# The fourth attention's result norms taken in three groups inside its steps, and a tile of the last layer cleared later

## What is computed

```
x = x + tanh(g_xattn[3]) * _L3_xattn_ref(_layernorm(x), ctx, ctx, mask, gamma, beta)
x = x + tanh(g_ffn[3])   * _L3_ffn_ref(_layernorm(x), Wg, bg, Wi, Wo, A, B)

def _L3_xattn_ref(q, k, v, mask, gamma, beta):
    logits = where(mask == 0, -9e15, q @ k.T / sqrt(d_k))
    x = softmax(logits) @ v
    mu, var = mean(x), mean((x - mu)**2)          # per token, over the 256 features
    return (x - mu) * rsqrt(var + 1e-5) * gamma + beta

def _L3_ffn_ref(x, ...):
    # softmax over 4 experts, the two best; one shared base x @ Wi and a rank-4 term per expert,
    # relu, @ Wo, weighted by the two scores
```

## Time and profile before

| | |
|---|---|
| median of 3 runs | 1665.69 us (1663.48 to 1671.44) |
| the profiled execution | 1655.67 us, of it 1653.8 us from the first to the last instruction |
| TensorE, busy share | 84% (weight loads 71%) |
| VectorE, ScalarE, GpSimd, busy share | 69%, 57%, 46% |
| instructions | 31758 |
| mean granted TensorE clock | 0.923 of full |

### The profile page before, as it was taken

How to read it: one execution, slowest core, us unless ns; L and a number is a source line. 1 busy time by engine, 2 the same in 40 slices (tenths; PEclk the granted TensorE clock), 3 DMA queues, 4 the chain that set the end, 5 groups by cost and what they waited for, 6 DMA issues and landing times. The chain is left out here.

```text
span 1653.8 us, 31758 instructions
## 1 busy us (share of the span) xinstructions
PE 1385.4 (84%) x10246; PEld 1178.8 (71%) x10246; DVE 1146.2 (69%) x2504; ACT 943.3 (57%) x2064; POOL 758.0 (46%) x799
## 2 busy tenths in 40 slices
PE   2599977999999999968986579999976976465898
PEld 0345565899999999944656479999875862254787
DVE  6457765678878888746966648888565758786554
ACT  3246652777777777736762337777624546574432
POOL 2323202467667667513312128888701770345444
PEclk8799998999999999979997689999998999675999
DMA  4000004365565566340004116767441000001001
GB/s 162 18 1 1 2 24 176 129 242 203 202 236 207 202 239 204 122 134 1 2 6 136 77 45 205 242 215 234 146 135 60 1 0 1 16 17 60 1 18 35
DMA packets 62367, 171.86 MB, mean 104 GB/s; under 512 B 11760, under 2 KB 43248, under 8 KB 53056
## 3 DMA queue, kind: packets, MB, share of 16 engines
q1 hardware_dynamic: 53440, 146.50, 25.3%
q0 software_dynamic: 8832, 24.13, 4.6%
HBM read 152.25 MB, written 18.35 MB: 103 GB/s over the span
## 5 line engine op out<-in xcount | busy, mean ns | idle before, releaser
L1721 POOL TENSOR_TENSOR l0m_e_DL<-l0m_e_DN,l0m_e_DH 128x256 fp32r<-128x256 f32 x184 | 184.1, 1006 | 119.3 <-ACT l0m_e_DH L1560 75.6
L1504 PE MATMUL PS<-l0m_e_CH,l0m_e_UH 128*128 128x256 f32 x736 | 210.9, 287 | 1.9 <-DVE l0m_e_CL L1654 1.9
L1504 PE MATMUL PS<-l0m_e_CH,l0m_e_UL 128*128 128x256 f32 x736 | 208.9, 284 | 0.0
L1504 PE MATMUL PS<-l0m_e_CL,l0m_e_UH 128*128 128x256 f32 x736 | 208.9, 284 | 0.0
L1626 DVE TENSOR_TENSOR l0m_e_UL<-l0m_e_U,l0m_e_UH 128x512 fp32r<-128x512 f32 x184 | 146.2, 795 | 10.4 <-ACT l0m_e_UH L1551 10.4
L1504 PEld LDWEIGHTS PS<-l0m_e_CH,l0m_e_UH 128*128 128x128 f32 x736 | 141.9, 193 | 2.2 <-ACT l0m_e_UH L1551 2.2
L1638 DVE SCALAR_TENSOR_TENSOR Z<-PS,l0m_e_BU,Z 128x256 f32<-128x256 f32 x184 | 88.7, 482 | 77.9 <-ACT Z L1568 74.8
L1504 PEld LDWEIGHTS PS<-l0m_e_CL,l0m_e_UH 128*128 128x128 f32 x736 | 142.1, 193 | 0.0
L1504 PEld LDWEIGHTS PS<-l0m_e_CH,l0m_e_UL 128*128 128x128 f32 x736 | 141.9, 193 | 0.0
L1568 ACT ACTIVATE Z<-PS,l0m_e_BU 128x256 f32<-128x256 f32 x184 | 87.6, 476 | 83.6 <-PE PS L1504 70.4
L1551 ACT CAST l0m_e_UH<-l0m_e_U 128x512 fp32r<-128x512 f32 x184 | 113.1, 615 | 0.0
(11 more groups left out here) (539 smaller groups left out, 4527.7 us busy)
## 6 DMA issues: line engine op xcount, KB each, us to landing
l0m_e_U<-in_l_up SPq DMA_DIRECT2D x23, 2048.0 KB
l0m_e_DN<-in_l_down SPq DMA_DIRECT2D x23, 1024.0 KB
l1m_e_U<-in_l_up SPq DMA_DIRECT2D x23, 1024.0 KB
l1m_e_DN<-in_l_down SPq DMA_DIRECT2D x23, 512.0 KB, 3.9
CTX<-in_ctx SPq DMA_DIRECT2D x2, 2048.0 KB, 10.3
l1a_GA<-results_by_choice SPq DMA_DIRECT2D x16, 256.0 KB, 5.6
l1m_c_GA<-results_by_choice SPq DMA_DIRECT2D x16, 256.0 KB, 4.8
Z<-in_l_b_rows SPq DMA_DIRECT2D x23, 128.0 KB
```

The lines of the kernel that those rows point to most:

```text
L1504: ins = nc.tensor.matmul(hb(f)[:, a * SLOTS:(a + 1) * SLOTS], w[:, f % RING, k, a, :], x[:, j, k, :], start=(p == 0), stop=(p == len(passe ...
L1721: nc.gpsimd.tensor_tensor(DL[:, f % RING, :], DN[:, j, f, :], DH[:, f % RING, :].bitcast(F32), ALU.subtract).then_inc(s_dl, 1)
```

## The change

In the attention, the norm of the result is taken in three groups, sequences 0 to 7, 8 to 11 and 12 to 15. The first two groups and the start of the third run inside the 22 steps:

| step | VectorE adds, at the end of the step | ScalarE adds, at the end of the step |
|---|---|---|
| 12 | scales of 0..7 | |
| 13 | | root of 0..7 |
| 14 | factors of 0..7 | |
| 15 to 18 | | hat of two of 0..7 in each step; in step 17 then the root of 8..11 |
| 16 | scales of 8..11, then gamma 0, 1 | |
| 17 to 19 | gamma of two of 2..7 in each (in 18 factors of 8..11 ahead of them) | step 19: hat of 8..11 |
| 20, 21 | step 20: scales of 12..15; gamma of two of 8..11 in each; step 21: then factors of 12..15 | |
| behind | statistics of X 0..11, gamma 12..15 between the first four, then statistics of 12..15 | root and hat of 12..15 |

In the last layer ONES is cleared before LO, and LO only once VectorE has normalised four sequences; `parts` waits for `s_one` to be 3.

```diff
+            LAST = ((0, 8), (8, 12), (12, 16))
...
+                        def hat(n, lo, hi):
+                            act.wait_ge(s_ok, n + 3)
+                            act.wait_ge(s_tr, hi)
+                            for b in range(lo, hi):
+                                nc.scalar.activation(Z[:, b, :], Y[:, b, :], ACT.Identity, bias=SMALL[:, 2, b:b + 1],
+                                                     scale=RSTD[:, b:b + 1]).then_inc(s_hat, 1)
...
-                        deviation(3, 0, B)
-                        act.wait_ge(s_ok, 3)
-                        for b in range(B):
-                            nc.scalar.activation(Z[:, b, :], Y[:, b, :], ACT.Identity, bias=SMALL[:, 2, b:b + 1],
-                                                 scale=RSTD[:, b:b + 1]).then_inc(s_hat, 1)
+                            if t == 13:
+                                deviation(3, *LAST[0])
+                            if 15 <= t < 19:
+                                hat(0, 2 * (t - 15), 2 * (t - 15) + 2)
+                            if t == 17:
+                                deviation(4, *LAST[1])
+                            if t == 19:
+                                hat(1, *LAST[1])
+                        deviation(5, *LAST[2])
+                        hat(2, *LAST[2])
...
+                        def scales(n):
+                            dve.wait_ge(s_ys, LAST[n][1])
+                            dve.wait_ge(s_za, LAST[n][1] // 2)
+                            row_scales(ch, s_var, *LAST[n])
+
+                        def factors(n):
+                            row_factors(dve, ch, s_sd, n + 3, s_ok, *LAST[n])
+
+                        def gamma(b):
+                            dve.wait_ge(s_hat, b + 1)
+                            nc.vector.tensor_tensor(Z[:, b, :], Z[:, b, :], GB[:, 0, :], ALU.mult).then_inc(s_gm, 1)
...
-                        dve.wait_ge(s_ys, B)
-                        row_scales(ch, s_var, 0, B)
-                        row_factors(dve, ch, s_sd, 3, s_ok, 0, B)
-                        for b in range(B + 3):
-                            if b < B:
-                                dve.wait_ge(s_hat, b + 1)
-                                nc.vector.tensor_tensor(Z[:, b, :], Z[:, b, :], GB[:, 0, :], ALU.mult).then_inc(s_gm, 1)
-                            if b >= 3:
-                                x_stats(b - 3)
+                            if t in (12, 16, 20):
+                                scales(t // 4 - 3)
+                            if t in (14, 18):
+                                factors((t - 14) // 4)
+                            if 16 <= t < 20:
+                                gamma(2 * (t - 16))
+                                gamma(2 * (t - 16) + 1)
+                            if t >= 20:
+                                gamma(8 + 2 * (t - 20))
+                                gamma(9 + 2 * (t - 20))
+                            if t == 21:
+                                factors(2)
+                        for b in range(12):
+                            x_stats(b)
+                            if b < 4:
+                                gamma(12 + b)
+                        for b in range(12, B):
+                            x_stats(b)
...
                         nc.gpsimd.memset(SC[:, :, :], -1.0).then_inc(s_one, 1)
+                        nc.gpsimd.memset(ONES[:, :], 1.0).then_inc(s_one, 1)
+                        pool.wait_ge(s_zd, 4)
                         nc.gpsimd.memset(LO[:, :, :, :], 0.0).then_inc(s_one, 1)
-                        nc.gpsimd.memset(ONES[:, :], 1.0).then_inc(s_one, 1)
...
-                            dve.wait_ge(s_one, 2)
+                            dve.wait_ge(s_one, 3)
```

## The result

The changed kernel took 1673.92 us (median of 18 executions, 1665.45 to 1680.23), the kernel before beside it 1666.74 us (18, 1661.99 to 1674.99). The ratio is 1.0033, 95% interval 1.0019 to 1.0047: 5.5 us slower, 3.2 to 7.8. Two more measurements of the same program gave 1.0041 (1.0024 to 1.0059) and 1.0026 (1.0005 to 1.0046). All three intervals lie above 1. On the prediction's base of 1665.69 us a ratio of 1.0033 makes 1671.2 us.

What follows compares the result with a forecast made beforehand. The prediction took VectorE, a queue of work with few waits from step 12 on, as the bound; +2.0 us (attention) and 0 (clear) on the median 1665.69 gave 1667.7 us, range 1659 to 1673.5.

Steps and rivals of the forecast that it cites:

- rival B: Attention, slower than the sum: three roots with loads and the exponential's load stand in full; +5.5 us, 1671.2; 17 in 100.
- Part 1: Attention's result norm in groups inside the steps: VectorE's queue grows +2.0 us, ends -3.9 and about +5.5.
- maximum of 12: Attention step 12, VectorE: aggregates and epsilon come first, so it starts near 1471.8 us, not 1471.29.
- exponential 13: Attention, ScalarE: held behind two table loads and a root, it starts near 1475.9 us; before, it started at 1473.51.
- maximum of 15: Attention, VectorE: its scores wait for ScalarE's copy; it starts near 1477.8 us, not 1475.44, 2.3 us late.
- the last block: End of the attention, VectorE: twelve statistics of X at 0.34 us each, with no hold and no wait.
- The split of the sum: VectorE's attention queue: common work unchanged, scales and factors +1.1, waits +0.2, holds +0.7; sum +2.0 us.
- fixed: Attention, VectorE: further groups' scales and factors (epsilon, reciprocal, product, dependent waits), 1.65 us before, 2.75 after, +1.1.
- holds: Attention: VectorE operations beside a GpSimd add end shortly after that add; 3.4 us before, 4.1 after, +0.7.
- Part 2: Last layer, moved clear of LO: epsilon falls from 1.95 to some 0.2 us, DMA still gates; 0 of 1.8 us gained.
- the step that ended the sum behind part 2: Last layer: beyond the moved clear, at 0 us, the forecast added nothing for it; total stayed +2.0 us.
- Rival A: Attention's steps take the norm for nothing, loads falling mostly into ScalarE's idle time: -3.9 us, 1661.8, or 1660.0; 23 in 100.

## Why the prediction was right, and where it was not

**Direction and class** came out as forecast: slower, by less than half a per cent. The size did not: +2.0 us was forecast, +5.5 measured. The 1671.2 us that this makes lie inside the 1659 to 1673.5 given, but near its upper end, and are to the tenth the price of rival B, which had 17 in 100. **Part 1**, the attention, was forecast at +2.0 and is +2.3 (28.31 - 26.03). Its steps hold one by one, counted from `y_stats(7)`: maximum of 12 at 1.19 us (forecast 1.1), exponential 13 at 5.36 (5.2), maximum of 15 at 7.38 (7.1); waits of 0.52, 0.78, 0.20, 0.74 and 0.74 us (0.4, 0.7, 0.3, 0.7, 0.8), and 0.33 for hat 12 (0.4); the last block is twelve statistics in one piece.

**The split of the sum** was off inside a good total. It booked +1.8 us of work (+1.1 fixed, +0.7 holds) and +0.2 of waits; the trace has +1.4 busy and +0.9 idle. The waits before were 2.9 us and not 3.6, so the sum let too much old waiting vanish against the new. The two errors partly cancel, and that part 1 came out within 0.3 us is in part luck. The split also hides the cause: without the root and its three loads the same groups are 0.5 us faster than before (25.52 against 26.03), while two loads alone cost 2.2 us in the old order and the three cost 2.8 in the new. Before, the tail's own load ran while VectorE aggregated (1478.73 to 1480.01; the add of epsilon that the root waits for starts only at 1480.41), so it was all but free.

**Part 2**, the clear at 0, is right: the epsilon fell to 0.17 us, the DMA still released the first turn.

**What failed** is the step that ended the sum behind part 2, where the rest of the last layer was taken as unchanged. Its work is unchanged, but the time that it spends at 1.2 GHz is not: +1.0 to +1.3 us in four of the five traces with this attention, +8 in one. This term had no place in the forecast, and the rivals did not have it either. B named +5.5 us, the measured size, but by loads standing in full, while exponential 13 was held by 2.6 us and the stretch grew by 2.3; that B's sum meets the measured ratio is chance. Rival A falls, since its covering of the loads by idle time did not happen. The Trainium skill gives 2.66 us for a change of table (ScalarE: Activation LUTs, What ACT_TABLE_LOAD costs). The traces here agree on its load, 1.28 us, but not on the whole: 1.30 us each. By the Trainium skill's figure the prediction put part 1 at +5.5, without showing the working, and +2.3 was measured.

**Left open:** why the clock meets the changed kernel's last layer otherwise, how often it stays low for those 20 us, and whether the three ratios (1.0026 to 1.0041) hold anything beyond that. What lies ahead of the attention varies by 18 us from trace to trace, so the few traces there are cannot say.

## What to carry to other kernels

Work that is moved from a tail into a pipeline can save only waits and holds of the engine that fills both, as far as this case shows; sum that engine's queue first, and see what the moved work brings along on the others. Here it brought two table loads into the chain of exponentials, and placing the root behind the last exponential, with one group fewer and a new order, took 4.1 us off the same stretch. A stretch of a trace that repeats within 0.2 us decides what eighteen timed executions can't; but it says nothing of what the change does elsewhere, so read the next stage as well.

## What the runs showed that I had not expected

The same last layer takes 156 to 164 us, by when TensorE's granted clock rises and whether it stays up. And the length of a pair of gamma and add depends on a backlog: with adds always waiting, each pair takes 0.86 us (13.73 / 16); where each add starts only when its gamma is done, the changed kernel's gammas 13 to 15 come every 1.15 us (1510.94 to 1512.09), since the next gamma is then held by that add, and the add behind it waits for the gamma:

```profile
1510.94 0.89 DVE L3112 TENSOR_TENSOR Z<-Z,l3a_GB 128x256 f32<-128x256 f32 x1
...
1512.09 0.89 DVE L3112 TENSOR_TENSOR Z<-Z,l3a_GB 128x256 f32<-128x256 f32 x1
```
